# Attention of a fused layer: the second choice's expert rows loaded plainly and added on VectorE, the first choice's still accumulated by a transfer

## The reference, cut to what matters

```python
xn = layernorm(x)
attn = softmax(causal(rope(q) @ rope(k).T * scale))       # per sequence, 64 features
o = attn @ v
z = o @ W_comp2lat.T
attention = z @ W_to_kv + z @ W_out_res.T + b_out_res
shared = silu(xn @ gate) * (xn @ up) @ down
routed = w1 * expert1(xn) + w2 * expert2(xn)              # top 2 of 16
out = x + attention + shared + routed
```

## Time and profile before

| | before |
|---|---|
| median of 3 runs | 1924.59 us (1923.59 to 1928.51) |
| profiled execution | 1919.11 us |
| its span | 1917.3 us |
| mean granted clock of TensorE | 0.973 of full speed |
| TensorE, VectorE, ScalarE, GpSimd busy | 92%, 60%, 39%, 36% |
| `attend` within the span | from about 1549 us to the end |

### The profile page before, as it was taken

One profiled execution on the slowest core, in us unless ns is written; L12 is line 12 of the kernel. 1 busy time (PEld: TensorE's weight loads), 2 busy tenths in 40 slices (PEclk: granted clock), 3 DMA queues, 4 the chain that ended last, 5 costly groups with the idle time before them and its releaser, 6 DMA issues. The chain is left out here.

```text
span 1917.3 us, 28075 instructions
## 1 busy us (share of the span) xinstructions
PE 1771.4 (92%) x8509; PEld 1407.6 (73%) x8509; DVE 1146.9 (60%) x2227; ACT 753.8 (39%) x1287; POOL 686.9 (36%) x646
## 2 busy tenths in 40 slices
PE   2799999999999995999999999999999969899998
PEld 1677777777777783777887777778878747677776
DVE  5677677777767652555555555555555346666665
ACT  2322222232222211333333343333333368677775
POOL 0644544554455444333333333333333211110110
PEclk8799999999999997999999999999999989999999
DMA  7667777666777526545545545545443259998884
GB/s 260 211 190 231 222 206 213 225 183 195 232 212 208 194 74 229 171 136 173 177 171 181 171 159 195 202 170 187 165 161 103 65 132 208 242 212 189 187 196 118
DMA packets 149582, 352.59 MB, mean 184 GB/s; under 512 B 19996, under 2 KB 41564, under 8 KB 149472
## 3 DMA queue, kind: packets, MB, share of 16 engines
q1 hardware_dynamic: 96924, 234.59, 37.1%
q0 software_dynamic: 43968, 104.91, 21.5%
q10 hardware_dynamic: 8580, 11.64, 2.2%
HBM read 208.30 MB, written 146.70 MB: 185 GB/s over the span
## 5 line engine op out<-in xcount | busy, mean ns | idle before, releaser
L1302 POOL DMA_INDIRECT expert_rows<-res,ids_all x143 | 149.6, 1046 | 460.9 <-ACT res L1135 450.8
L1250 DVE TENSOR_REDUCE mx<-emb 128x1 f32<-128x512 f32 (+3 forms) x288 | 174.8, 642 | 108.2 <-PE emb L1056 79.7
L69 PE MATMUL egu<-w,rT_0h 128*128 x576 | 186.4, 405 | 6.0 <-SPq L986 6.0
L69 PE MATMUL egu<-w,rT_1h 128*128 x568 | 182.4, 402 | 0.0
L877 POOL DMA_INDIRECT token_list<-tok,slot x128 | 125.6, 981 | 150.4 <-DVE slot L644 114.5
L1499 ACT ACTIVATE ex<-sc 128x1024 f32<-128x1024 f32 (+4 forms) x176 | 144.4, 821 | 65.5 <-PE sc L1443 58.3
L1227 DVE TENSOR_TENSOR eh<-egu,esg 128x256 f32<-128x256 f32 x143 | 60.7, 424 | 182.7 <-ACT esg L1125 182.7
L1297 POOL DMA_INDIRECT rows<-xn_scratch,rows_all x143 | 138.6, 970 | 70.2 <-issue 44.8
L1568 POOL DMA_DIRECT2D base<-expert_rows x32 | 41.0, 1329 | 294.9 <-DMA base<-expert_rows 175.4
L1125 ACT ACTIVATE esg<-egu 128x256 f32<-128x256 f32 x143 | 54.9, 384 | 195.9 <-PE egu L69 193.1
L1442 PE MATMUL sc<-qh,khl 128*128 128x512 f32 (+3 forms) x288 | 114.0, 396 | 18.0 <-DVE last L1548 12.8
(11 more groups left out here) (282 smaller groups left out, 4551.7 us busy)
## 6 DMA issues: line engine op xcount, KB each, us to landing
w<-expert_parts SPq DMA_DIRECT2D x64, 768.0 KB, 7.8
base<-expert_rows POOLq DMA_DIRECT2D x32, 1024.0 KB, 10.8
expert_parts<-ew_h SPq DMA_DIRECT2D x32, 768.0 KB, 5.4
expert_parts<-ew_l SPq DMA_DIRECT2D x32, 768.0 KB, 6.7
x<-x SPq DMA_DIRECT2D x16, 1024.0 KB, 6.3
xn_scratch<-xn SPq DMA_DIRECT2D x16, 1024.0 KB, 6.6
base_scratch<-xb SPq DMA_DIRECT2D x16, 1024.0 KB, 8.5
base<-base_scratch SPq DMA_DIRECT2D x16, 1024.0 KB, 8.9
```

Of the source, the lines that this page charges most:

```text
L69: mm = pe.matmul(dst, w, m, start=(first and i == 0), stop=(last and i == len(terms) - 1))
L1250: dve.tensor_reduce(mx[n % 2][:, j, c:c + 1], mb[g % 2][:, 0:width], AX.X, ALU.max).then_inc(m_red, 1)
L1302: pool.indirect_dma_start(parts_d[:, :], bass.IndirectOffsetOnAxis(ap=ids_all[:, t:t + 1], axis=0), res[t % 2][:, :], None, bounds_check=2 ...
```

## The change

Only the first choice's rows are still accumulated by a transfer. The second choice's rows are loaded plainly by SyncE, one block of 128 rows (256 KB) at a time, into six new buffers `second`, and VectorE adds each block to `base` in `combine`, ahead of the wait for the projection. `base` has three buffers instead of four. SyncE's program is no longer three rounds per group: it walks the steps as the other engines do, loads block m + 6 when the combine of block m is done, loads the base of group k+2 at the second projection of group k and stores group k at its fourth.

```diff
--- before.py
+++ after.py
@@ -1324,7 +1324,7 @@
         sb = lambda name, shape, dt=F32: ctx.enter_context(nc.sbuf_tensor(name, shape, dt))
         ps = lambda name, banks=1: ctx.enter_context(nc.psum_tensor(name, [P, 512 * banks], F32))
         sem = lambda name: ctx.enter_context(nc.semaphore(name))
-        NE, NP, NQ, NB = 2, 4, 3, 4
+        NE, NP, NQ, NB, NS = 2, 4, 3, 3, 6
         LAG = 3
         SCALE = C ** -0.5
 
@@ -1337,16 +1337,18 @@
         oT = [[sb(f"oT_{i}{c}", [P, GROUP], F32R) for c in "hl"] for i in range(2)]
         lr = [sb(f"lr_{i}", [P, 2 * GT]) for i in range(2)]
         base = [sb(f"base_{i}", [P, GT, D]) for i in range(NB)]
+        second = [sb(f"second_{i}", [P, D]) for i in range(NS)]
 
         sc = [ps(f"sc{i}", 2) for i in range(2)]
         ob = [ps("ob0"), ps("ob1")]
         pj, nb = ps("pj"), ps("anb")
 
-        q_in, base_in, one_in, two_in, out_st = [[sem(f"{name}{i}") for i in range(count)] for name, count in
-                                                 (("q_in", NQ), ("base_in", NB), ("one_in", NB), ("two_in", NB), ("out_st", NB))]
+        q_in, base_in, one_in, second_in, out_st = [[sem(f"{name}{i}") for i in range(count)] for name, count in
+                                                 (("q_in", NQ), ("base_in", NB), ("one_in", NB), ("second_in", NS), ("out_st", NB))]
         blank, ready, q_high, q_low = sem("a_blank"), sem("a_ready"), sem("q_high"), sem("q_low")
         s_done, e_done, pv_done, low_done = sem("s_done"), sem("e_done"), sem("pv_done"), sem("low_done")
         o_hi, o_ev = sem("o_hi"), sem("o_ev")
+        s_ev = sem("s_ev")
         l_done, l_ev, p_done, p_ev = sem("al_done"), sem("l_ev"), sem("p_done"), sem("p_ev")
 
         base_g = base_d.rearrange("(g j p) d -> g p j d", j=GT, p=P)
@@ -1372,6 +1374,7 @@
         first, final = [rows[0] for rows in group_steps], [rows[-1] for rows in group_steps]
 
 
+        ends = {final[k]: k for k in range(NG)}
         finish = {final[k] + LAG: k for k in range(NG)}
         project_at, free = {}, 0
         for k in range(NG):
@@ -1411,22 +1414,36 @@
                 sp.wait_ge(p_ev, GT * k + GT)
                 sp.dma_start(out_g[ORDER[k]], base[k % NB][:, :, :]).then_inc(out_st[k % NB], 16)
 
+            def store_rows(k, j):
+                sp.wait_ge(p_ev, GT * k + j + 1)
+                sp.dma_start(out_g[ORDER[k]][:, j, :], base[k % NB][:, j, :]).then_inc(out_st[k % NB], 16)
+
+            def load_second(m):
+                k, j = divmod(m, GT)
+                after(sp, p_ev, m - NS + 1)
+                sp.dma_start(second[m % NS][:, :], parts_g[NG + ORDER[k]][:, j, :]).then_inc(second_in[m % NS], 16)
+
             for k in range(2, NQ):
                 load_queries(k)
-            for k in range(2):
+            for k in range(NB):
                 load_base(k)
-            for k in range(NG):
-                if k + 2 < NG:
-                    load_base(k + 2)
-                if k + NQ < NG:
-                    load_queries(k + NQ)
-                if k:
-                    store_out(k - 1)
-            for j in range(GT):
-                sp.wait_ge(p_ev, GT * (NG - 1) + j + 1)
-                sp.dma_start(out_g[ORDER[NG - 1]][:, j, :], base[(NG - 1) % NB][:, j, :]).then_inc(out_st[(NG - 1) % NB], 16)
+            for m in range(NS):
+                load_second(m)
+            for i in range(TAIL):
+                if i in ends and ends[i] + NQ < NG:
+                    load_queries(ends[i] + NQ)
+                if i in project_at:
+                    k, j = project_at[i]
+                    if GT * k + j + NS < GT * NG:
+                        load_second(GT * k + j + NS)
+                    if k == NG - 1:
+                        store_rows(k, j)
+                    elif j == GT - 1:
+                        store_out(k)
+                    elif j == 1 and 0 < k <= NG - NB:
+                        load_base(k + NB - 1)
             for b in range(NB):
-                sp.wait_ge(out_st[b], 16 * NG // NB + (16 * (GT - 1) if b == (NG - 1) % NB else 0))
+                sp.wait_ge(out_st[b], 16 * len(range(b, NG, NB)) + (16 * (GT - 1) if b == (NG - 1) % NB else 0))
 
         @block.tensor
         def _(pe):
@@ -1537,8 +1554,11 @@
                     dve.wait_ge(l_done, k + 1)
                     dve.reciprocal(lr[k % 2][:, :], nb[:, 0:2 * GT]).then_inc(l_ev, 1)
                     dve.wait_ge(l_ev, k + 1)
-                    dve.wait_ge(two_in[k % NB], 16 * (k // NB + 1))
-                row = base[k % NB][:, j, :]
+                    dve.wait_ge(one_in[k % NB], 16 * (k // NB + 1))
+                row, m = base[k % NB][:, j, :], GT * k + j
+                dve.wait_ge(second_in[m % NS], 16 * (m // NS) + 16)
+                dve.tensor_tensor(row, row, second[m % NS][:, :], ALU.add).then_inc(s_ev, 1)
+                dve.wait_ge(s_ev, m + 1)
                 dve.wait_ge(p_done, GT * k + j + 1)
                 dve.scalar_tensor_tensor(out=row, in0=pj[:, :], scalar=lr[k % 2][:, 2 * j:2 * j + 1], in1=row,
                                          op0=ALU.mult, op1=ALU.add).then_inc(p_ev, 1)
@@ -1559,18 +1579,13 @@
 
         @block.gpsimd
         def _(pool):
-            def add_rows(k, c):
-
-                if c == 0:
-                    pool.wait_ge(base_in[k % NB], 16 * (k // NB) + 16)
-                else:
-                    pool.wait_ge(one_in[k % NB], 16 * (k // NB + 1))
-                pool.dma_start(base[k % NB][:, :, :], parts_g[c * NG + ORDER[k]], accum_op=ALU.add
-                               ).then_inc((one_in, two_in)[c][k % NB], 16)
+            def add_rows(k):
+
+                pool.wait_ge(base_in[k % NB], 16 * (k // NB) + 16)
+                pool.dma_start(base[k % NB][:, :, :], parts_g[ORDER[k]], accum_op=ALU.add).then_inc(one_in[k % NB], 16)
 
             for k in range(NG):
-                add_rows(k, 0)
-                add_rows(k, 1)
+                add_rows(k)
 
 
 def rope_tables():
```

## The result

The changed kernel takes 1957.88 us in the median of four runs (1955.06 to 1967.76), the kernel before 1926.55 us in the median of four (one more than stood in the table above): the ratio is 1.016, 95% interval 1.0136 to 1.0185. It is slower, as forecast, but by 31 us and not by 17, and it lies 2 us beyond the upper end of the range.

The account below looks back on a forecast made before the run. TensorE was taken to bound the last stage; 10.7 + 0.5 + 0.1 + 4.6 + 1 = 17 us more gave 1936 us profiled, 1941.5 as a median. Range 1927 to 1956, lower end drawn to 1919 by the no-change case.

Parts of the forecast that it names:

- The added add: 64 VectorE additions ahead of the combines, each combine 0.71 us later: 10.7 us, plus 0.5 and 0.1 us.
- of two tight hand-overs only the first pays: Combine to next projection on TensorE: 16 hand-overs pay 0.71 us less their slack, 10.7 us together.
- The removed half: Sixteen 1 MB accumulates leave GpSimd's queue: DMA engine load falls from 83 to about 70%; no compute engine waited for it.
- The moved queue: SyncE's new order puts query loads behind stores or base loads: new waits 18.4 us, net +4.6 us.
- Its range: For the moved queue's +4.6 us: -7 us with stores at 4.3 us, +12 with 9 us each.
- The clock: Low granted clock after TensorE's holes, seven holes instead of five: +1 us, between -5 and +10.
- Three buffers: `base` with three buffers instead of four costs nothing: at least 32 us of cover against 8.9 + 10.8 us.
- every combine pays: Rival: the add makes VectorE the second half of each step's loop, 43 us instead of 10.7, 1974; chance 0.07.
- The rival of the other side, lighter traffic that wins: Query loads land in time: 1919 or, with a third of tight hand-overs regained, 1915; no change 0.18, faster 0.12.

Follow-up runs that it names:

- e6: The kernel before with the query loads of a round issued ahead of its base load; 1922.1 us, ratio 0.9922 to the kernel before.
- e7: e1 with the add left out, so the second choice is missing from the output; 1920.9 us, ratio 0.9922 to the kernel before.
- e1: The changed kernel with SyncE issuing the query loads one step earlier; 1915.9 us, ratio 0.9959 to the kernel before.
- e3: The kernel before plus 64 additions of a zeroed buffer to the base row, transfers unchanged; 1949.0 us, ratio 1.0055 to the kernel before.
- e10: The changed kernel with its accumulates left out, so the first choice is missing from the output; 1927.3 us, ratio 1.0018 to the kernel before.
- e11: e1 with each add moved one step ahead of its combine; 1903.5 us, ratio 0.9893 to the kernel before.
- e8: e1 with the second choice's row added twice; 1934.7 us, ratio 1.0059 to the kernel before.

## Why the prediction was wrong, point by point

The parts can be walked through in stage lengths: from before to e6 -12.3 us (queries first), to e7 -2.8 (half the accumulates gone, the loads plain, SyncE walking the steps, no add), to e1 +12.6 (the adds), to the changed kernel +37.3 (its own order on SyncE). Together they are the 34.8 us. By the ratios of the medians the same steps are -15, 0, +7 and +39 us, together 31. The largest one is the same in both.

- **The added add**: right. 685 ns for 684, 271.9 us of VectorE work for 274; at the tail VectorE still waits 1.21 us before each of the last three combines. Forecast 10.7 and 0.5 us, measured 12.6 (stage) or 7 (ratio) by e7 and e1, and 10.7 by e3. That of two tight hand-overs only the first pays held in the sum of the waits: 8.7 us more in e1 than in e7. The count of pieces was off: eleven more (19 for 8), where I had named some twenty.
- **The removed half**: right in that nobody had waited for it. An accumulate takes the engines the same time as before (24.9% of 404 us for 16.78 MB, 6.0 us per MB). That accumulates would land in under 10 us was wrong, they took 11.2.
- **The moved queue**: the step that failed. The groups were right: waits for 5, 7, 8, 9, 10, 13 and 15, none for 6, 11, 12 and 14. The size was not. I took 7.1 us from a store's issue to the queries: the store's median of before and 1 us for the queries. That median comes from stores that had the queries ahead of them, and of which only four of fifteen were issued 1 to 4 us behind an accumulate (those took 8.5 to 14 us, the upper values of the range that I had quoted). In the new order eight of fifteen are, and land in 9.8 to 12.5 us. Ahead of the queries of groups 7, 13 and 15 the store is issued 1 to 2 us before the accumulate and lands in 5.4 to 6.1, but then the queries behind it meet the accumulate and are there 8 to 10 us after the store's issue. Measured were 11.4 us for group 5 and 11.6 for group 9, and the waits were 6.5, 5.0, 2.6, 8.0, 1.6, 3.6 and 2.9 us, 30.2 in sum for the 18.4 forecast. The whole miss is in the five groups whose queries stand behind a store: 26.1 us for 13.1. Groups 8 and 10 came to 4.1 us for 5.3. With no accumulate beside them (e10) the queries were there in 6.1 to 6.4 us, under the 7.1. I read each queue by itself and did not ask when the accumulates would start in the new order; the landing time of 5.7 us for a base load, with two steps left to the store, would have told it.
- **Its range** was too narrow by its own reading. With stores at 9 us instead of 6.1 each of five waits grows by 2.9 us, 14.5 in all, of which TensorE by the same share loses 13: +17 or +18 us where I wrote +12.
- **What the order cost**: 37.3 us in the changed kernel and 12.3 in the one before, so +25 us (24 by the ratios) where the forecast for queries and clock together was +5.6. By the windows of e1 and e6 some 16 us of the 25 are idle time of TensorE (forecast +4.6) and some 9 are slower matmuls (forecast +1).
- The Trainium skill's fit (DMA: Bandwidth & Descriptors, anatomy of one DMA) is for a transfer issued by GpSimd and gives, as an estimate, 4.4 us for the 1 MB store alone and 5.0 us for store and queries. The quickest stores of before took 4.3 us, those of e10 5.2 us in the median, and e10's queries were there after 6.1 us. With an accumulate beside them the queries of the changed kernel took 8 to 11.6 us, and the measurement decides.
- **The clock**: forecast +1 us, measured 11.0 us more busy time for the same matmuls. The runs with few and short holes, e1 and e11, have 3.4 us and none of the lower level; the changed kernel has 37.5 us in six stretches, each beside a hole behind a late query. I had priced the number of holes, not their length: the longest hole, 8.75 us up to 1738.59, goes with the longest stretch, 13.7 us at 0.50 from 1731.9 on.
- **Three buffers**: nothing, as forecast. VectorE waited for no transfer.
- **The rivals**: that every combine pays is excluded by e3, e7 and e8. The rival of the other side, lighter traffic that wins, needed the queries in time, and e1 shows that it was open: with them in time the change is 0.4% faster than the kernel before. But e6 gives the kernel before 0.8 to 0.9% with both its accumulates, so the gain was the order's.

## What to carry to other kernels

When a change moves bulk transfers within a queue, list for every small load that an engine soon needs what will stand ahead of it, and what runs on the other queues at that moment; a median landing time of the old order is no price for the new one. Put the small urgent loads first: here the place of one load in the program was worth 37 us. An added instruction on an engine with idle time costs where it stands in front of a hand-over, so put it on a step where nobody waits behind it.

## What was not expected of the hardware

- A 1 MB store lands in 5.2 us with no accumulating transfer beside it and in 9.8 in the changed kernel (medians of 15), though the accumulate moves only 1 MB itself; and in the changed kernel it matters which comes first: 9.8 to 12.5 us where the accumulate is issued 1 to 4 us ahead of the store, 5.4 to 6.1 where it is issued 1 to 2 us behind it. That does not carry over to every order: in e6 two stores issued 0.6 and 1.3 us ahead of an accumulate, but 0.4 us behind a base load, took 12.8 and 11.4 us.
- A hole of TensorE costs more than its length. Against e1 the changed kernel has 25.0 us more idle time and, with the same matmuls, 12.3 us more busy time. Its holes of 6.33, 5.29 and 8.75 us stand beside stretches of 6.8, 6.8 and 13.7 us at the lower clock level; the 1536 matmuls took 347.7 us instead of 335.4.
